# Gate logits from three half-precision products instead of one single-precision product

## What is computed

```
xf = layernorm(x)                                   # (1024, 512)
gate_logits = einsum('td,ed->te', xf, gate_w)       # (1024, 8)
gate_scores = sigmoid(gate_logits + balance_bias)
topk_scores, topk_idx = top_k(gate_scores, 2)
topk_scores = topk_scores / (topk_scores.sum(-1) + 1e-6)
```

## Time and profile before

| | |
|---|---|
| median of 3 runs | 589.7 us (588.83 to 590.61) |
| the profiled execution's own time | 589.92 us |
| its span in the profile | 588.0 us |
| busy in it: PE, DVE, ACT, POOL | 506.1, 391.0, 285.9, 113.1 us |
| clock granted to TensorE, mean over the span | 0.935 of full speed |

### The profile page before, as it was taken

One profiled execution on the slowest core, in us unless ns is written; L12 is line 12 of the kernel. 1 busy time (PEld: TensorE's weight loads), 2 busy tenths in 40 slices (PEclk: granted clock), 3 DMA queues, 4 the chain that ended last, 5 costly groups with the idle time before them and its releaser, 6 DMA issues.

```text
span 588.0 us, 11090 instructions
## 1 busy us (share of the span) xinstructions
PE 506.1 (86%) x3601; PEld 294.6 (50%) x3602; DVE 391.0 (67%) x876; ACT 285.9 (49%) x449; POOL 113.1 (19%) x89
## 2 busy tenths in 40 slices
PE   5799999999989899886630699999999999999993
PEld 3664657474657576645330344445445444544441
DVE  2889778937977969698886566666563736673330
ACT  0652868686256464675720345454443525652120
POOL 1212114102232030300471001211211121121112
PEclk9799999999989989897855779999999999999998
DMA  8992505000008994125288157887585776744222
GB/s 326 390 382 87 216 1 215 2 1 2 1 0 303 379 382 172 37 80 208 90 299 294 44 174 223 267 255 237 107 262 132 218 214 154 232 93 90 54 54 37
DMA packets 54961, 98.74 MB, mean 168 GB/s; under 512 B 25072, under 2 KB 26256, under 8 KB 50832
## 3 DMA queue, kind: packets, MB, share of 16 engines
q1 hardware_dynamic: 23984, 74.81, 35.9%
q10 hardware_dynamic: 26640, 13.73, 9.5%
q0 software_dynamic: 4304, 9.77, 7.8%
HBM read 63.36 MB, written 29.43 MB: 158 GB/s over the span
## 4 chain that ended last, share of the span: by engine, by line
PE 67%; DVE 10%; issue 10%; ACT 5%; POOL 3%; DMA 3%; SPq 0%; ACTq 0%; POOLq 0%; DVEq 0%
PE bank L691 20%; PE bank L709 19%; PE bank L343 7%; PE bank L511 4%; PE bank L495 2%; PE bank L425 2%; PE bank L455 2%; PE bank L405 2%; PE bank L361 2%; PE bank L476 1%; PE bank L545 1%; ACT ctxT_region L737 1%; DMA routed_rows<-shared,ints 1%; POOL small L1544 1%; PE bank L604 1%
## 5 line engine op out<-in xcount | busy, mean ns | idle before, releaser
L691 PE MATMUL bank<-wbuf,ctx_region 128*128 x504 | 117.8, 393 | 6.3 <-issue 5.3
L1400 DVE SCALAR_TENSOR_TENSOR wbuf<-ctx_region,wbuf 128x2048 f32 (+1 forms) x28 | 62.9, 2288 | 31.9 <-ACT wbuf L876 31.9
L1642 POOL DMA_INDIRECT out<-misc,ints x21 | 38.6, 1840 | 230.2 <-ACT misc L957 175.0
L691 PEld LDWEIGHTS bank<-wbuf,ctx_region 128*128 128x128 f16 x504 | 49.4, 101 | 66.9 <-issue 15.5
L876 ACT ACTIVATE wbuf<-ctx_region 128x2048 f32 (+1 forms) x28 | 51.9, 1902 | 28.6 <-issue 26.2
L1544 POOL TENSOR_TENSOR small<-small 128x2 f32<-128x2 f32 (+2 forms) x25 | 27.7, 1109 | 190.8 <-DVE small L1030 184.2
L709 PE MATMUL bank<-wbuf,actT 128*128 x264 | 58.8, 379 | 1.0 <-DVE actT L1504 1.0
L976 ACT ACTIVATE ctxT_region<-bank 128x512 f32<-128x512 f32 x42 | 25.1, 597 | 69.6 <-PE bank L691 69.6
L709 PE MATMUL bank<-wbuf,xn 128*128 x240 | 53.4, 379 | 0.0
L511 PE MATMUL bank<-ctx_region,wbuf 128*128 128x256 f16 x384 | 45.2, 280 | 4.3 <-DVE ctx_region L1159 3.4
L511 PEld LDWEIGHTS bank<-ctx_region,wbuf 128*128 128x128 f16 x384 | 38.0, 100 | 12.0 <-DVE ctx_region L1159 4.1
(11 more groups left out here) (214 smaller groups left out, 823.4 us busy)
## 6 DMA issues: line engine op xcount, KB each, us to landing
ctx_region<-in_experts SPq DMA_DIRECT2D x28, 1024.0 KB, 5.4
routed_rows<-ctxT_region SPq DMA_DIRECT2D x1, 16900.0 KB, 50.6
ctx_region<-in_ctx SPq DMA_DIRECT2D x8, 1536.0 KB, 8.8
ctx_region<-routed_rows ACTq DMA_DIRECT2D x23, 260.0 KB, 3.6
wbuf<-in_experts SPq DMA_DIRECT2D x4, 1024.0 KB, 4.9
out<-x ACTq DMA_DIRECT2D x8, 256.0 KB, 2.5
x<-in_x SPq DMA_DIRECT2D x1, 1536.0 KB, 14.3
wbuf<-in_wqT SPq DMA_DIRECT2D x4, 256.0 KB, 4.3
```

Source lines behind the costliest of these rows:

```text
L691: mm = nc.tensor.matmul(bank[half][:, :], xgT[:, b, x_part, k * P:(k + 1) * P], w16[:, ds(at + (w_part + k * EH + half * 512), 512)], star ...
L1400: nc.vector.scalar_tensor_tensor(w16[:, ds(at + (LOW + n * PIECE), PIECE)], src_[:, piece], W_SCALE, w16[:, ds(at + (HIGH + n * PIECE), PI ...
L1642: nc.gpsimd.indirect_dma_start(out, bass.IndirectOffsetOnAxis(idx[:, slot_no:slot_no + 1].bitcast(U32), axis=0), y_out[:, slot_no, :], Non ...
```

## The change

The turned features become two f16 tiles: ACT's copy out of PSUM now writes the high part (the same instruction with an f16 output), and a new DVE function `turned_low` writes the low part, the difference of bank and high part, one instruction per tile. The gate's weights are cut once into `gate16`, by two DVE instructions behind `cut_self_low(3)`, ahead of the loop over pairs. `logits` takes three passes, so 12 products per tile in place of 4, and waits for the low part (`xfT_lo`) in place of the high part (`xfT`). `logits_out` divides by 256 as it adds the bias. The two counts of `bo_cut` are given to the semaphore `bvo`, with the values waited for moved up by one.

```diff
             def logits(pair):
+                if pair == 0:
+                    pe.wait_ge(s["sw_lo"], 6)
                 if pair + 2 < PAIRS:
                     pe.wait_ge(s["sq"], 2 * pair + 6)
                 for t in range(2):
-                    pe.wait_ge(s["xfT"], 2 * pair + t + 1)
+                    pe.wait_ge(s["xfT_lo"], 2 * pair + t + 1)
                     for k in range(KC):
-                        mm = nc.tensor.matmul(bank[LOGIT_BANK[pair] + t][:, 0:E], xfT[:, k, t * P:(t + 1) * P], gate_w[:, k, :],
-                                              start=(k == 0), stop=(k == KC - 1))
+                        for x_part, w_part in PASSES:
+                            mm = nc.tensor.matmul(bank[LOGIT_BANK[pair] + t][:, 0:E], xfT[:, x_part, k, t * P:(t + 1) * P],
+                                                  gate16[:, w_part, k, :], start=(k == 0 and x_part + w_part == 0),
+                                                  stop=(k == KC - 1 and x_part == 1))
                     mm.then_inc(s["z_ps"], 1)
...
+            def turned_low(pair):
+
+                for t in range(2):
+                    tile_at = slice(t * P, (t + 1) * P)
+                    dve.wait_ge(s["xfT"], 2 * pair + t + 1)
+                    nc.vector.tensor_tensor(xfT[:, 1, :, tile_at], bank[6 + t][:, :].rearrange("p (k t) -> p k t", k=KC),
+                                            xfT[:, 0, :, tile_at], ALU.subtract).then_inc(s["xfT_lo"], 1)
+
             def logits_out(pair):
...
-                    nc.vector.tensor_tensor(z[:, tile, :], bank[LOGIT_BANK[pair] + t][:, 0:E], row("balance"), ALU.add)\
-                        .then_inc(s["z"], 1)
+                    nc.vector.scalar_tensor_tensor(z[:, tile, :], bank[LOGIT_BANK[pair] + t][:, 0:E], 1.0 / W_SCALE, row("balance"),
+                                                   ALU.mult, ALU.add).then_inc(s["z"], 1)
...
             cut_self_low(3)
+            nc.vector.tensor_scalar(gate16[:, 0], gate_w[:, :, :], W_SCALE, None, ALU.mult).then_inc(s["sw_lo"], 1)
+            dve.wait_ge(s["sw_lo"], 5)
+            nc.vector.scalar_tensor_tensor(gate16[:, 1], gate_w[:, :, :], W_SCALE, gate16[:, 0], ALU.mult, ALU.subtract)\
+                .then_inc(s["sw_lo"], 1)
             for pair in range(PAIRS):
                 last = pair + 1 == PAIRS
                 softmax(pair)
+                if pair:
+                    turned_low(pair - 1)
                 if last:
                     choose(0)
                 if pair:
...
             place(1)
+            turned_low(PAIRS - 1)
             logits_out(PAIRS - 1)
```

More of the change, by code:

```diff
@@ L73 @@
 left_ve left_rstd left_n left_ps left_T
-qkb_ps qkb bqk bias_const bias_const_ps left_bias m1_ps m1_hi m1_lo m2_ps m2_hi m2_lo bvo_ps bvo bo_cut x1_hi x1_lo x2a_hi x2a_lo
+qkb_ps qkb bqk bias_const bias_const_ps left_bias m1_ps m1_hi m1_lo m2_ps m2_hi m2_lo bvo_ps bvo x1_hi x1_lo x2a_hi x2a_lo
 cx_ve cx_rstd cx_shift cx_n0 cx_n1 cxT_ps cxT left_cols
@@ L78 @@
 rotated k_exp sv_ps sv ss_ps softmax_step s_sub s_exp s_pT p_cols ao_ps ao_hi ao_lo sy_ps x_post x_plus_sbo
-ln4_ve ln4_rstd xf xf_hi xf_lo xfT_ps xfT z_ps z out_init
+ln4_ve ln4_rstd xf xf_hi xf_lo xfT_ps xfT xfT_lo z_ps z out_init
 route rt_sel rt_cnt_ps rt_exp rt_slots rt_map zrow_fill zrow xs_zero rows_set scattered
@@ L114, in program @@
         ident16 = sb("ident16", [P, P], F16)
+        gate16 = sb("gate16", [P, 2, KC, E], F16)
         two_rows = sb("two_rows", [64, P], F16)
@@ L217, in program @@
         v = c.take(2, 2, D)
-        xfT = c.take(KC, 2 * P)
+        xfT = c.take(KC * 2 * P).bitcast(F16).rearrange("p (a k t) -> p a k t", a=2, k=KC)
         c = Carve(ctxT_region, 0, 2 * CC * BT * KEYS)
@@ L489, in context_result @@
                 if pair == 0:
-                    pe.wait_ge(s["bo_cut"], 2)
+                    pe.wait_ge(s["bvo"], 3)
                 for t in range(2):
@@ L856, in features_out @@
                     act.wait_ge(s["xfT_ps"], 2 * pair + t + 1)
-                    nc.scalar.copy(xfT[:, :, t * P:(t + 1) * P],
+                    nc.scalar.copy(xfT[:, 0, :, t * P:(t + 1) * P],
                                    bank[6 + t][:, :].rearrange("p (k t) -> p k t", k=KC)).then_inc(s["xfT"], 1)
@@ L1228, in _ @@
                     dve.wait_ge(s["bvo"], 1)
-                    nc.vector.tensor_scalar(bo16[:, :], bo, W_SCALE, None, ALU.mult).then_inc(s["bo_cut"], 1)
-                    dve.wait_ge(s["bo_cut"], 1)
+                    nc.vector.tensor_scalar(bo16[:, :], bo, W_SCALE, None, ALU.mult).then_inc(s["bvo"], 1)
+                    dve.wait_ge(s["bvo"], 2)
                     nc.vector.scalar_tensor_tensor(bo16[32:64, :], row("bo")[32:64, :], W_SCALE, bo16[32:64, :],
-                                                   ALU.mult, ALU.subtract).then_inc(s["bo_cut"], 1)
+                                                   ALU.mult, ALU.subtract).then_inc(s["bvo"], 1)
                 if pair + 1 < PAIRS:
```

## The result

| | before | changed |
|---|---|---|
| median of the runs | 588.73 us (22 runs, 585.13 to 591.7) | 590.89 us (22 runs, 589.43 to 595.81) |
| ratio | | 1.0054 (95% interval 1.0032 to 1.0075) |
| span of the profiled run | 588.0 us | 592.6 us |
| PE busy in it | 506.1 us | 498.0 us |
| DVE busy in it | 391.0 us | 396.8 us |

The change makes the kernel slower by 0.54%, some 3 us, and by 4.6 us between the spans of the two profiled executions. PE lost 8 us of work against the earlier trace rows, and DVE gained 5.8 us. The forecast was +4.35 us. The profiled execution of the changed kernel took 594.46 us, and only 3 of its 22 runs took longer; so the two profiles together show more than the medians do.

What follows compares the result with a forecast made beforehand. DVE's chain with PE's answers was taken to bound each pair. The terms 1.7 + 1.35 + 1.3 + 0 gave +4.35 us on 589.9 us profiled, 594.3, stated as a 594.1 us median; range 591.3 to 597.3 us.

Steps and rivals of the forecast that it cites:

- Rival A: Gate products in pairs and behind the loop: PE sets the pace, so 6.4 us faster, 583.3 us; chance 0.04.
- The marks: Turned features starting on PE: pair 2 at 242.1 us against 240.41, pair 3 some 3.0 us later, behind the loop 4.35.
- three signs of being wrong: Time between two pairs' turned features not growing; line 1353's successor unshortened and later; `values` slowing with DVE waiting for ACT.
- Pair 1, +1.7: Second logits read in pair 1: 1.28 us of DVE's low part plus 0.4 us waiting for PE.
- rival B: PE late too: lower clock slows `values` in pairs 1 and 2, perhaps pair 3; up to +8.4, middle 596.5 us; chance 0.16.
- Pair 2, +1.35: Second logits read in pair 2: as pair 1, less the 0.36 us DVE waited there before.
- rival C: Scores of pairs 1 and 2: less PE idle time, higher clock gives back up to 1.2 us each, 591.7 us; chance 0.12.
- Pair 3, +1.3: Pair 3: DVE's low part adds 1.3 us; PE, out of `attend` about 1 us later, matters less.
- The price of the products: PE's half-precision gate products: 24 take 0.74 us, about 0.4 us a tile; at the lower clock some 0.65 us a tile.
- Behind the loop, 0: Second read comes 1.35 us later, but POOL holds line 1353 until 301.42 us anyway: 0, or 1.35 if POOL moved.
- The gate cuts, 0 behind cover: Two DVE setup instructions ahead of pair 0's softmax fit DVE's 4.88 us idle time: cost 0, at most 1.4 us uncovered.
- the ring: A pair's period: nearly all DVE, the rest PE's answer; DVE work added between softmax and last normalisation counts in full.

Runs made afterwards that it cites:

- e4: Kernel before, with only one of four single-precision gate products per tile; 595.37 us, but routing differs, so only stages up to the last turned features can be compared.
- e1: Changed kernel without the low part and the pass that uses it (high part alone, logits less precise); 590.37 us, ratio 1.003 to the kernel before.
- e3: Changed kernel with each low part computed twice, one after the other; 595.98 us, ratio 1.0129 to the kernel before.
- e2: Changed kernel with the low part moved ahead of the softmax in pairs 1 and 2; 588.13 us, ratio 0.9988 to the kernel before.
- e7: e2 with the third and fourth piece of expert 1's weights held until the first routed rows are there; 585.21 us, ratio 0.9938 to the kernel before.
- e9: Changed kernel without low part and its pass, expert 1's third and fourth weight pieces held until the first routed rows; 585.37 us, ratio 0.9949 to the kernel before.
- e12: e9 with pair 3's sixteen products per token tile made four times over, as filler for PE; 586.69 us, ratio 0.9952 to the kernel before.
- e6: Changed kernel with the third and fourth quarter of expert 1's weights loaded only after the first rows landed; 588.0 us, ratio 0.9992 to the kernel before.
- e5: Kernel before, with the third and fourth quarter of expert 1's weights loaded only after the first rows landed; 583.17 us, ratio 0.9907 to the kernel before.

## Why the prediction came out right

- **The direction and its reason: right.** PE's saving was worth nothing (e4: 0.3 us over three pairs), DVE's added work nearly its full length in pairs 1 and 3 (e1, e3). Where it stands matters: with the same instructions placed early (e2) the kernel is 0.66% faster than the changed one. Rival A is refuted by e4 for the three pairs.
- **The range.** It was 591.3 to 597.3 us, on a kernel before of 589.7 us (3 runs). The median of 22 runs of that kernel is 588.73, and the changed kernel's 590.89 lies 0.4 us under the range; 589.7 times the measured ratio is 592.9, inside it.
- **The marks.** Forecast were +1.7 us at the turned features in pair 2, +3.0 in pair 3 and +4.35 behind the loop; measured are +2.91, +2.91 and +3.85, with the 0.83 of the first mark in each. Two of the three signs of being wrong came: the interval of pair 2 did not grow, and `values` slowed in pair 1 with DVE waiting for ACT ahead of L1295.
- **Pair 1, +1.7: right by +1.62** at the second read (DVE 2.45 us late there, 0.83 at the pair's first mark). Then rival B's part came on top: `values` 7.03 us, ACT late, DVE idle 0.37 us ahead of L1295. +2.08 at the mark; the "about 0.5 reaches DVE" of rival B was 0.46.
- **Pair 2, +1.35: +1.32 from the softmax's end to the second read, but 0 at the mark.** Here rival C came: L546 took 1.95 us in place of 3.29, so that DVE was through its softmax 1.31 us earlier after the mark, and this gave the 1.32 back. The step that failed is the judgment that B and C were alternatives to the forecast. Each happened once, in different pairs. Over both pairs I had 3.05 and it was 2.08.
- **Rival C's reason is not shown.** PE's idle time ahead of these scores did fall, from 2.88 to 1.87 us, as rival C had it. But in e7, e9 and e12 it is 2.88 or 2.89 us and the scores take 1.95 or 1.96 us all the same, in e9:

```profile
242.52 1.96 PE L548 MATMUL bank<-ctx_region 128*32 128x128 f32 x64
```

  In e9 the second group of eight products in `attend` (L587) then took 3.26 us in place of 1.89, and nothing was gained (29.81 us); in e12 it kept 1.89, and pair 2 took 28.15 us. `values` shows the same: behind 2.34 us of idle time it took 7.03 us in pair 1, behind 2.33 us in pair 2 it kept 5.34. So neither the slow `values` nor the fast scores follow from the length of the idle time alone; that each came where it did was luck, and the two nearly cancelled (+0.46 and -1.31).
- **Pair 3, +1.3: +0.94.** Too high by 0.36: the low part brought 1.18 us of lateness, not 1.28, and 0.27 came back in one small instruction of `place` (0.49 us at line 1391 before, 0.22 now).
- **The price of the products: 0.74 expected, 0.75 found** where both tiles are ready (e2). The 0.97 us of the changed kernel holds a pause of 0.23 us between the tiles, in which PE waits for the second low part. At the lower clock I took 0.65 us a tile, 1.3 for both; it was 1.08 with a pause of 0.29. The clock hardly touches these products: they start 25 ns apart at a granted clock of 1.00 (pair 1) and 27 ns apart at 0.50 (pair 3), the single-precision ones 112 and 213 ns. So my doubling of the price at the lower clock, in pair 3 and in rival A, was wrong for them. The Trainium skill, FP8 and Floating Point Precision, TensorE Precision Notes, would have three passes cost three quarters of 1.85 us, 1.39. No run shows that: for these 8 columns it was 0.75.
- **Behind the loop, 0: right.** The read came 1.56 us later against its own mark's lateness, L1366 took 0.86 in place of 2.41 us, and from the mark to POOL's last scatter it is 19.11 us against 19.08. The Trainium skill, SBUF — State Buffer, Who interferes with whom, has it so, and the trace agrees: L1366, with two SBUF inputs, ended at 305.44 us, 0.16 us after POOL's pair, as line 1353 did before (301.58 and 301.42). The low part L1342, with one input from PSUM, took 1.28 us there and 1.25 in the pairs; only its last 0.26 us lay beside POOL's pair.
- **The gate cuts, 0 behind cover: right, with the wrong price.** I gave 0.69 us for each at most; they took 1.25 and 1.21 us for 32 elements a partition. POOL's four instructions of L1605 (171.42 to 178.36 us) ran beside them; whether they are the reason was not tested. The 4.88 us of idle time covered it, 2.47 was left.
- **What I left out altogether** is the landing of the last scatters and the first row load. It moved by +2.1 us in the profiled pair, and the loop over row tiles, which I had as unchanged, gave 1.4 back, so the sum of +4.35 met the profiled +4.6 partly by luck: the ring gave 3.0 of it, 0.8 was there at the first mark, the landing 2.1, the loop -1.4.
- **The medians:** the change cost 3.2 us by the ratio (1.9 to 4.4) where 4.35 were forecast. With the load held in both (e6 to e5) it is 4.8, of which about half is the low part (e6 to e9); the cause of the other half is open.

## What to carry to other kernels

Before a faster product on one engine is bought with work on another, ask which of the two had idle time at that very place; and where the work must be added, put it where its engine waits anyway: here the same instructions cost 2 us of pair 1 behind the softmax and nothing ahead of it. The clock can take time in one stage and give it back in the next, and in this kernel the length of the idle stretch ahead didn't tell which. Before a busy time is scaled with the clock, look whether it holds a wait. When medians and profiles don't tell the same story, look for a transfer with no deadline that was released early: a wait of two lines was worth more than the whole change.

## What was not expected of the hardware

- While 1 MB pieces of weights were in flight, small scatters and a row load took up to 3 us longer each: 7.2 against 4.1 us for the last scatter, 5.66 against 2.7 us for the load. From the turned features to the first rows the DMA engines were busy for 0.84 of the time at 290 GB/s before, 0.78 at 272 GB/s with the change and 0.75 at 262 GB/s in e5; the busiest slices of the page have 390 GB/s.
- 24 f16 products of 8 columns took 0.75 us, and they start 25 ns apart at a granted clock of 1.00 and 27 ns at 0.50; in e1 sixteen of them took 0.55 us in pair 1 and 0.57 behind the loop, at 1.00 and 0.50. The 16 single-precision ones took 1.85 and 3.58 us, a factor of 1.94.
- Two DVE instructions of 128 by 32 took 1.25 and 1.21 us beside POOL's work, where one of 128 by 32 in `choose` (L1373) took 0.18 us. POOL's work was beside them in every run that has them, so its part is not shown.
- DVE stood idle for 0.46 us at one place in pair 0 in all ten profiled kernels with the changed code and in none of the four with the code of before. The cause is open.
- Executions of one kernel fell into two groups by mean granted clock (e9: 0.934 to 0.936 and 0.942 to 0.945), and 2 to 5 us go with it (e9: 586.3 to 588.8 against 583.3 to 584.4).
